# Expert routing weights repeated through memory instead of by a TensorE product, and the shared experts' tile first in a group

## The reference, cut to what matters

```python
B, S, H = (2, 128, 128);  E, F = (16, 64);  G, TOPK_G, TOPK = (4, 2, 4)
def _gate(x, w_gate):
    scores = jax.nn.sigmoid(x @ w_gate.T)
    sv = scores.reshape(T, G, E // G)
    group_scores = jax.lax.top_k(sv, 2)[0].sum(-1)
    top_groups = jax.lax.top_k(group_scores, TOPK_G)[1]
    ...
    _, idx = jax.lax.top_k(masked, TOPK)
    w = jnp.take_along_axis(scores, idx, axis=1)
    w = w / (w.sum(-1, keepdims=True) + 1e-06) * ROUTE_SCALE
    return (w, idx)
combine = (jax.nn.one_hot(idx, E, dtype=x.dtype) * weights[..., None]).sum(1)
g = jax.nn.silu(jnp.einsum('th,efh->tef', x, w1_e))
u = jnp.einsum('th,efh->tef', x, w3_e)
routed = jnp.einsum('tef,ehf,te->th', g * u, w2_e, combine)
shared = _swiglu(x, w1_s, w3_s, w2_s)
...
x = x + _L1_ffn_ref(_layernorm(x, axis=-1), ...)
```

## Time and profile before

| | |
|---|---|
| median of three runs | 1436.89 us (1435.78 to 1447.15) |
| the profiled execution's own time | 1445.3 us |
| its span | 1443.5 us |
| last stage, from its first product | 1197.2 us to the end |
| busy share: PE, DVE, ACT, POOL | 84%, 70%, 58%, 39% |
| mean granted clock of TensorE | 0.944 |

### The profile page before, as it was taken

One profiled execution on the slowest core, in us unless ns is written; L12 is line 12 of the kernel. 1 busy time (PEld: TensorE's weight loads), 2 busy tenths in 40 slices (PEclk: granted clock), 3 DMA queues, 4 the chain that ended last, 5 costly groups with the idle time before them and its releaser, 6 DMA issues. The chain is left out here.

```text
span 1443.5 us, 41003 instructions
## 1 busy us (share of the span) xinstructions
PE 1219.2 (84%) x12535; PEld 772.9 (54%) x12535; DVE 1014.3 (70%) x3805; ACT 834.4 (58%) x1625; POOL 570.0 (39%) x825
## 2 busy tenths in 40 slices
PE   2899999999498888888598788888888546999998
PEld 1455555555255555555386465665555333655665
DVE  2477778776366666666465388899998728887885
ACT  1477777776277777777233477777776342333321
POOL 4667777772222222222010255566654521211120
PEclk9999999999599999999799799999999566999999
DMA  5000000000000000000000388888888221000000
GB/s 169 1 2 2 0 0 0 0 2 2 1 2 2 0 0 0 0 0 1 1 0 1 84 218 220 215 224 225 227 225 227 65 64 54 8 9 16 8 8 15
DMA packets 152051, 82.92 MB, mean 57 GB/s; under 512 B 6874, under 2 KB 150372, under 8 KB 151700
## 3 DMA queue, kind: packets, MB, share of 16 engines
q1 hardware_dynamic: 151428, 79.65, 20.4%
q0 software_dynamic: 528, 2.10, 0.5%
HBM read 43.72 MB, written 38.01 MB: 57 GB/s over the span
## 5 line engine op out<-in xcount | busy, mean ns | idle before, releaser
L764 POOL TENSOR_TENSOR rr<-ms_eps,minus_half 128x16 f32<-128x16 f32 x64 | 185.0, 2908 | 80.3 <-DVE ms_eps L987 80.3
L1120 DVE TENSOR_REDUCE rowmax<-psum 128x4 f32<-128x768 f32 x128 | 122.7, 959 | 60.8 <-PE psum L2074 60.8
L506 PE MATMUL psum<-identb,stacks 128*128 128x128 bf16 x1544 | 123.6, 225 | 19.0 <-DVE X L542 8.0
L1330 DVE CUSTOM_DVE_ANT_0 summed<-psum,pos_score 128x128 f32<-128x128 f32 x512 | 118.0, 286 | 24.0 <-PE psum L2273 15.8
L1026 DVE TENSOR_REDUCE rowmax<-psum 128x4 f32<-128x512 f32 x128 | 88.2, 689 | 63.8 <-PE psum L1940 62.6
L1886 ACT ACTIVATE pos_rows<-psum 128x512 f32<-128x512 f32 x72 | 43.0, 597 | 143.9 <-PE psum L2448 137.0
L2315 PE MATMUL psum<-consts,summed 128*128 128x128 f32 x512 | 85.6, 292 | 46.4 <-DVE summed L1336 46.2
L1776 ACT ACTIVATE probsT<-psum 128x512 f32<-128x512 f32 x128 | 77.4, 605 | 77.7 <-PE psum L597 47.5
L506 PEld LDWEIGHTS psum<-identb,stacks 128*128 128x128 bf16 x1544 | 95.3, 100 | 48.3 <-issue 23.8
L371 POOL TENSOR_TENSOR rstd<-vareps,minus_half 128x4 f32 (+1 forms) x24 | 25.3, 1055 | 195.0 <-DVE vareps L362 195.0
L824 POOL TENSOR_TENSOR rest<-staged,stacks 128x128 f32<-128x128 f32 x32 | 13.7, 429 | 220.5 <-ACT stacks L489 220.5
(11 more groups left out here) (264 smaller groups left out, 3182.2 us busy)
## 6 DMA issues: line engine op xcount, KB each, us to landing
skew<-pos_rows SPq DMA_DIRECT2D x128, 258.0 KB, 4.0
pos_score<-skew SPq DMA_DIRECT2D x128, 256.0 KB, 3.9
X<-in_x_dram POOLq DMA_DIRECT2D x1, 2048.0 KB, 12.4
ctxT<-in_ctx_dram SPq DMA_DIRECT2D x1, 2048.0 KB, 11.2
out_dram<-X SPq DMA_DIRECT2D x8, 256.0 KB, 2.3
w_up<-in_L_ffn_w_e_dram SPq DMA_DIRECT2D x2, 512.0 KB, 4.7
y_rows<-hidden SPq DMA_DIRECT2D x4, 256.0 KB, 2.3
y_rows<-qT SPq DMA_DIRECT2D x4, 256.0 KB, 2.3
```

Source lines behind the costliest of these rows:

```text
L506: last = pe.transpose(turned[:, t, :], stacks[:, which, 2 * t:2 * t + 2, :].rearrange("s h k -> s (h k)"), identb[:, :])
L764: pool.tensor_tensor(out=rr[:, par, i * H:(i + 1) * H], in0=ms_eps[:, i * H:(i + 1) * H], in1=minus_half[:, 0:H], op=ALU.pow).then_inc(A.r ...
L1120: dve.tensor_reduce(rowmax[:, par, PT * r:PT * r + PT].rearrange("s (h b) -> s b h", b=2), B.max_space, AX.X, ALU.max, negate=True).then_i ...
L1330: last = dve.tensor_tensor_reduce(summed[:, r % 2, p, :], P.score_bank[r % 2][:, p, :], pos_score[:, par, r * PT + p, :], 1.0, -3.0e38, AL ...
```

## The change

Ahead of the row tiles, the order of a group's tiles changes: position p = 0 is the shared tile and p = 1 to 8 are the routed ones. The split in parts, its transposes, the spread products and their table go. The weights of a group are kept in one f32 array `combine` of 128 tokens by 64 (four blocks' experts) and PE transposes it in one f32 product at the end of the group before (L2461). ACT copies that (L1898, 128 x 128). SP writes the 64 rows of 128 to memory (L740, 32 KB), waits for it, and reads for each routed tile two rows of 512 weights back, each of them onto 64 partitions (L747), so 2 x 128 KB for a tile. The tiles' weights lie in a ring of four buffers in SBUF (`weight_rows`, in space of `pos_score` that is free in this stage). `a` (L1526) multiplies by them. The routing's last steps, up to the product that makes `combine`, all stand ahead of tile 8.

```diff
-        ROUTE_STEPS = 27
-        ROUTE_AT = {2: (0, 8), 3: (8, 15), 4: (15, 16), 5: (16, 17), 7: (17, 18), 8: (18, ROUTE_STEPS + 1)}
+        ROUTE_STEPS = 23
+        ROUTE_AT = {2: (0, 8), 3: (8, 15), 4: (15, 16), 5: (16, 17), 7: (17, ROUTE_STEPS)}
+        def tile_of(p):
+            return TILES - 1 if p == 0 else p - 1
...
+            def write_weights(g, gpar):
+                wait(sp, F.cT, g + 1)
+                sp.dma_start(combine_rows[gpar].rearrange("e (k s) -> (e k) s", k=4), combineT[0:4 * EX, gpar, :]).then_inc(F.written, 16)
+            def read_weights(g, gpar, e):
+                wait(sp, F.a, g * (TILES - 1) + e - 3)
+                for half in range(2):
+                    sp.dma_start(weight_rows[half * FW:(half + 1) * FW, e % 4, :],
+                                 combine_rows[gpar][2 * e + half, :].partition_broadcast(FW)).then_inc(F.weights[e % 4], 16)
...
+            def weigh_group(g, gpar, left):
+                write_weights(g, gpar)
+                wait(sp, F.written, 16 * (g + 1))
+                for e in range(TILES - 1):
+                    read_weights(g, gpar, e)
+                    if e == 4 and (not isinstance(g, int) or g > 0):
+                        write_out(g - 1)
... DVE
-                dve.tensor_copy(spreadb[0:3 * EX, :, :], spread[:, :, :]).then_inc(F.cast, 1)
...
-                        wait(dve, F.spread, routed + 1)
+                        wait(dve, F.weights[(p - 1) % 4], F.weights_before + 32 * (2 * g + (p - 1) // 4 + 1))
                         wait(dve, F.y, n - 1)
-                        dve.tensor_tensor(hidden_a[:, par, :], gated[:, :], F.combine_bank, ALU.mult).then_inc(F.a, 1)
+                        dve.tensor_tensor(hidden_a[:, par, :], gated[:, :], weight_rows[:, (p - 1) % 4, :], ALU.mult).then_inc(F.a, 1)
... ACT
-                    for k in range(TILES):
-                        tile(g, par, k)
-                        if left >= 1 and k == 0:
+                    for p in range(TILES):
+                        tile(g, par, p)
+                        if isinstance(g, int) and g == 0 and p == 1:
+                            save_combine(0, 0)
+                        if left >= 1 and p == 0:
                             save_group(g + 1, 1 - par)
-                        if k == 1:
-                            save_combine(g, par)
-                        if left >= 1 and k == 1:
+                        if left >= 1 and p == 1:
                             gate(g + 1)
+                    if left >= 1:
+                        save_combine(g + 1, 1 - par)
... PE
+                    wait(pe, F.route, (g + 1) * ROUTE_STEPS)
+                    wait(pe, F.scores, g + 1)
+                    pe.transpose(F.gate_bank[:, 0:S], combine[:, :], ident).then_inc(F.cT_ps, 1)
...
-                    first_up(g, par, 1)
-                    turn_combine(g)
-                    second_up(g, par, 1)
-                    spread_weights(g, par, 0)
+                    for p in range(1, TILES):
+                        first_up(g, par, p)
+                        second_up(g, par, p)
+                        if not later and p == 1:
+                            turn_combine(0)
+                        down(g, par, p - 1)
+                        if left >= 1 and p == 1:
+                            gate(g + 1, 1 - par)
                     if left >= 1:
-                        gate(g + 1, 1 - par)
-                    for k in range(1, TILES):
-                        if k > 1:
-                            first_up(g, par, k)
-                            second_up(g, par, k)
-                        down(g, par, k - 1)
-                        if k < TILES - 1:
-                            spread_weights(g, par, k)
+                        turn_combine(g + 1)
```

More of the change, by code:

```diff
@@ L636, in decoder @@
         LOADS_D = 12 * 16
[L637 removed]
+        LOADS_F = 8 * 16
         @block.sync
@@ L1438, in experts @@
                 flat = masked[:, :, :, :].rearrange("s k g e -> s k (g e)")
-                part = [parts3[:, :, i * EX:(i + 1) * EX] for i in range(3)]
                 ROUTE = [
@@ L1484, in route, with tile @@
                             wait(dve, F.ties, 2 * (g + 1))
-                        if k == ROUTE_STEPS - 4:
+                        if k == ROUTE_STEPS - 1:
+                            wait(dve, F.zeroed, 1)
                             wait(dve, F.cT_ps, g)
                         step(g, k, ROUTE[k])
-                    if first <= ROUTE_STEPS < last:
-                        wait(dve, F.route, (g + 1) * ROUTE_STEPS)
-                        dve.tensor_copy(part[2], combine[:, :, :]).then_inc(F.split, 1)
-                def tile(g, gpar, k):
-                    n, par = g * TILES + k, (gpar + k) % 2
-                    routed = g * (TILES - 1) + min(k, TILES - 1)
+                def tile(g, gpar, p):
+                    n, par = g * TILES + p, (gpar + p) % 2
                     wait(dve, F.silu, n + 1)
                     wait(dve, F.h3, n + 1)
-                    if k < TILES - 1:
+                    if p == 0:
+                        wait(dve, F.y, n - 1)
+                        dve.tensor_tensor(hidden_a[:, par, :], silu[:, par, :], F.h3_bank[par], ALU.mult).then_inc(F.gated, 1)
+                    else:
+                        routed = g * (TILES - 1) + p - 1
                         wait(dve, F.a, routed)
@@ L1872, in gate @@
                     wait(act, F.gate, g + 1)
-                    wait(act, F.split, g)
+                    wait(act, F.route, g * ROUTE_STEPS)
                     act.activation(scores4[:, :, :].rearrange("s k e -> s (k e)"), F.gate_bank[:, 0:4 * EX], ACT.Sigmoid)\
@@ L1878, in save_combine, with tile @@
                     wait(act, F.cT_ps, g + 1)
-                    act.activation(combineT[:, gpar, :, :].rearrange("e b s -> e (b s)"), F.gate_bank, ACT.Copy)\
-                       .then_inc(F.cT, 1)
-                def tile(g, gpar, k):
-                    n, par = g * TILES + k, (gpar + k) % 2
+                    wait(act, F.written, 16 * (g - 1))
+                    act.activation(combineT[:, gpar, :], F.gate_bank[:, 0:S], ACT.Copy).then_inc(F.cT, 1)
+                def tile(g, gpar, p):
+                    n, par = g * TILES + p, (gpar + p) % 2
                     wait(act, F.h1, n + 1)
@@ L2438, in turn_combine @@
                 def turn_combine(g):
-                    wait(pe, F.split, g + 1)
-                    for k in range(4):
-                        last = pe.matmul(F.gate_bank[:, k * S:(k + 1) * S], parts3[:, k, :], identb[:, :], start=True, stop=True)
-                    last.then_inc(F.cT_ps, 1)
-                def first_up(g, gpar, k):
-                    n, par = g * TILES + k, (gpar + k) % 2
+                    wait(pe, F.route, (g + 1) * ROUTE_STEPS)
+                    wait(pe, F.scores, g + 1)
@@ L2463, in down @@
-                def down(g, gpar, k):
-                    n, par = g * TILES + k, (gpar + k) % 2
-                    if k == 0:
+                    pe.matmul(F.h3_bank[par], w_up3[:, tile_of(p), :], x, start=True, stop=True).then_inc(F.h3, 1)
+                def down(g, gpar, p):
+                    n, par = g * TILES + p, (gpar + p) % 2
+                    if p == 0:
                         wait(pe, F.x, g)
-                    if k < TILES - 1:
-                        wait(pe, F.a, g * (TILES - 1) + k + 1)
+                        wait(pe, F.gated, n + 1)
@@ L2469, in down @@
                     else:
-                        wait(pe, F.gated, n + 1)
+                        wait(pe, F.a, g * (TILES - 1) + p)
                     for b in range(4):
-                        last = pe.matmul(F.y_bank[:, b * D:(b + 1) * D], hidden_a[:, par, b * S:(b + 1) * S], w_down[:, k, :],
-                                         start=(k == 0 and b == 0), stop=(k == TILES - 1 and b == 3), skip_group_check=True)
+                        last = pe.matmul(F.y_bank[:, b * D:(b + 1) * D], hidden_a[:, par, b * S:(b + 1) * S], w_down[:, tile_of(p), :],
+                                         start=(p == 0 and b == 0), stop=(p == TILES - 1 and b == 3), skip_group_check=True)
```

80 lines of the change are left out of this document (34 added, 46 removed).

## The result

| | before | changed |
|---|---|---|
| median of 20 runs | 1437.78 us (1429.57 to 1447.15) | 1448.68 us (1442.34 to 1460.38) |
| ratio | 1 | 1.0081, 95% interval 1.0058 to 1.0104 |
| span of the profiled execution | 1443.5 us | 1441.5 us |
| start of the last stage in it | 1197.2 us | 1182.4 us |
| last stage in it | 246.3 us | 259.1 us |

The changed kernel is slower by 0.8%. Inside the stage the profiles do show it, 12.7 us in this one pair; the medians differ by 10.9, and the interval of the ratio is some 8 to 15 us.

What follows compares the result with a forecast made beforehand. DVE's pace bounds a group's middle, PE's order the transition. Three written-out groups at +1.25 us, four loop groups at +2.53, -2.2 and -0.8 sum to +10.9, giving 1448 us; range 1441 to 1456 as summed, 1433 to 1482 with rivals.

Steps and rivals of the forecast that it cites:

- The bound: Middle of a group goes at DVE's pace, 3.17 us a tile against PE's 2.83; PE's order decides the transition.
- The transition: From one group to the next, PE's new order takes 5.33 us against 6.66: -1.33 us a group.
- The five steps ahead of the last tile: Routing's five steps now stand in front of the last tile's DVE product: +1.18 us a group.
- The contention: `a` reads SBUF twice beside POOL's two long products: +1.3 us a group, between bounds of 1.0 and 1.65.
- The rule on it: DVE instruction with two SBUF inputs, coming later, is blocked for all of GpSimd's; the term would be 1.65 us.
- The gate: Gate's product behind the first down-product delays ACT's SiLU: +0.55 us in a written-out group, +1.83 in the loop.
- The weights' way: Way through memory takes about 6.8 us, wanted after 6.2; the rest lies under the gate's delay; 0 at stage's start.
- The loop-back: Between groups 3 and 4 an unexplained 3.36 us wait of the residual gets mostly hidden: -2.2 us once.
- D: Rival: PE's clock falls in the new gaps, once in each of seven groups: 1461 us, chance 0.10.
- Rival C: No contention between `a` and POOL, so 1.3 us falls away seven times: 1439 us, chance 0.12.
- rival B: Repeated reads of weights bind by bytes, 4.1 us a tile, a group about 35 us: 1481 us, chance 0.18.
- Rival E: Faster: POOL doesn't collide and ACT has its table early, 1430 us, or about 1410 at PE's pace; set at 1424, chance 0.12.

Runs made afterwards that it cites:

- e5: The kernel before, with POOL's two long products of a group cut from 1024 to 16 elements a row: 1430.55 us, ratio 0.9960.
- e4: The kernel before, with `a` reading its second factor from a fixed piece of SBUF instead of PSUM, no weights transferred: 1447.27 us, ratio 1.0083.
- e1: The changed kernel, with the two waits of ACT's gate in the other order inside the loop: 1441.91 us, ratio 1.0031 to the kernel before.
- e3: The changed kernel, with POOL's two long products cut to 16 elements a row: 1422.58 us, ratio 0.9916 to the kernel before.
- e6: The changed kernel, with each read of weights made twice and `a` waiting for both: 1456.75 us, ratio 1.0147 to the kernel before.
- e9: As e8, with two transfers for a tile's weights again, one for each half of the partitions: 1409.24 us, ratio 0.9806 to the kernel before.
- e8: The changed kernel with ranking ties on DVE, gate and its table load earlier, layernorm and last ranking steps moved, one weights transfer a tile: 1570.29 us.

## Why the prediction was right, point by point

The forecast was 1448 us, +11; measured were 1448.68, +10.9. The terms, from the starts of the DVE product in the two profiles, whose stages differ by 12.7:

| stretch | before | changed | difference | forecast |
|---|---|---|---|---|
| stage's start to group 1 | 47.83 | 51.52 | +3.69 | +1.25 |
| group 1 (written out) | 27.90 | 29.71 | +1.81 | +1.25 |
| groups 2 to 5 (loop) | 118.24 | 125.17 | +6.93 | +10.1 - 2.2 |
| group 6 (written out) | 26.89 | 28.28 | +1.39 | +1.25 |
| group 7 to the end | 25.48 | 24.39 | -1.09 | -0.8 |
| sum | 246.3 | 259.1 | +12.7 | +10.9 |

- **The bound.** Right: DVE's order of work set the pace, and taking 1.8 us of products a group from PE gave PE idle time. e5 shows the limit of that statement: when DVE's stretch of a group lost 1.59 us, PE became the bound and took 0.63 of it back.
- **The transition.** Right: 5.33 forecast, 5.38 to 5.77 measured in the loop and 5.61 in group 1, with PE waiting 0.94 at the transpose in group 2. Group 6 was shorter, 4.94.
- **The five steps ahead of the last tile.** Right in place; they run from 1288.50 to 1289.70, 1.2 us.
- **The contention.** Right in mechanism, and in size for six groups of seven: the two long `a` less what step 16 and the layernorm no longer lose come to 1.3 in groups 0 and 1 and 1.4 in groups 2 to 5, where 1.3 was taken; e4 alone gives 1.31 to 1.37. Mis-sized is group 6, which the sum counts like the others: no layernorm follows there, and it is 2.3. In all that is 10.7 instead of 9.1. The reading behind the lower bound, that 80% of an overlap is lost, was wrong: it came from instructions that met the last microsecond of POOL's product. An `a` that meets it early waits it out and ends 0.55 behind it, so of overlaps of 1.60 and 1.79 us it loses 1.46 and 1.65, all but 0.14. To land between the two bounds was luck.
- **The rule on it.** The Trainium skill (page "SBUF — State Buffer", section "Who interferes with whom") has the later instruction blocked for the whole of the other. That fits the long `a` better than 80% does, though the 1.65 that the prediction makes of it is 0.2 to 0.3 more than groups 0 to 5 show. The prediction leaves out a condition: the section lets an instruction with a single SBUF input go free only outside DVE's 2-port modes. The layernorm's has a single tensor input, X, and four of them took 1.89 beside POOL and 1.11 with POOL's products cut (e5). So with the rule as the prediction words it the trace does not agree; in which mode they ran no run here shows.
- **`gated` to `a`.** A term that I didn't have: in the loop these two stood 0.88 apart, with 0.19 of waiting, and now stand 0.72 apart in all but one tile. Over the six routed tiles behind a group's first that is 0.8 us back in a loop group. In the written-out groups, where most stood 0.71 to 0.8 apart before, it is 0.1 to 0.2.
- **The gate.** Right: 3.81 us in group 1, 5.14 to 5.49 in the loop (3.85 and 5.13 forecast); e1 shows that the load's place is what makes the difference.
- **The weights' way.** Right within a group (0.39 late, hidden); wrong at the stage's start, which I put at 0 without working it out: 3.92 us of waiting, and the first row of the table is 2.4 over its forecast. Up to 1.0 of that is the low clock of PE there, by the two waits for it.
- **The loop-back.** Right in kind, too small: groups 3 and 4 took 2.0 and 1.1 us over group 2 before, 3.1 in all where 2.2 was taken, and neither does now.
- **The rivals.** A fall of the clock in the groups' new gaps (D) is not seen: it is 1.00 in the windows of groups 1 to 7 of the changed kernel. Only in group 0 is it low, as shown above. Rival C is out by e3 and e4, rival B by e6. Rival E was wrong for the change as it stands, since its two conditions, no meeting with POOL and a table in time, don't hold; e9 fulfils them, moves the layernorm and the end of the ranking besides, and reaches 1409, near the 1410 that it gave for PE's pace.

So the loop groups that no loop-back touches, 2 and 5, were hit as a sum: they grew by 2.56 each, and 2.53 was forecast. Inside it single terms came out some tenths larger, and the closer pairs of products paid for that. The hit of the whole is partly luck. In the profiles the start was 2.4 us and group 1 was 0.6 too small, the loop-back about 1 too small on the other side, and in group 6 the contention and the transition missed in opposite directions; that leaves 12.7 against 10.9, and the medians happen to differ by 10.9.

## What to carry to other kernels

Ask, before an operand moves from PSUM to SBUF, which GpSimd instructions run at that moment: the DVE instruction with two SBUF inputs stood until POOL's had ended, and showed as busy while it stood. A change that relieves an engine which is nearly, but not quite, the bound pays only after the engine ahead of it has been relieved too: the same edit cost 13 us in the profiled stage (11 between the medians) with POOL's products in place, and gained some 4 in the stage without them. And a wait that moves ahead of a table load can cost the load, here 1.2 us a loop group (e1): look at what the order of two waits puts between them and the instruction.

## What the runs showed of the hardware

A transfer of 256 KB with an outermost dimension of two rows, each repeated on 64 partitions, took 5.12 us, at a DMA share of 0.13 to 0.17; as two transfers of one row on 64 partitions each they landed in 2.9 us (median). The Trainium skill has the rule (page "DMA: Bandwidth & Descriptors", section "Rules for kernel authors"): the number of engines that a transfer uses is taken from the slowest dimension of its access patterns, so a small one confines it to as many engines. e8 agrees: two of sixteen are a share of 0.125, and 0.13 was measured where nothing else moved. The same section advises one transfer of 128 partitions in place of two of half the partitions; here, where the halves have different sources and the one transfer had two rows outermost, the measurement says the opposite, 1570 us against 1409. One transfer with a longer outermost dimension was not tried.

The table loads of ACT took 1.28 us each, and the sigmoid began 1.30 after its load did.
